# The last message pass of a two-layer graph transformer on one core: its softmax weights read from a PSUM bank instead of SBUF

## The reference

```
def _gat_conv(x, W, a_src, a_dst, b, src, dst, n):
    xw = x @ W
    e = jax.nn.leaky_relu((xw @ a_src)[src] + (xw @ a_dst)[dst], 0.2)
    m = jax.ops.segment_max(e, dst, num_segments=n)
    ex = jnp.exp(e - m[dst])
    s = jax.ops.segment_sum(ex, dst, num_segments=n)
    alpha = ex / (s[dst] + 1e-16)
    agg = jax.ops.segment_sum(alpha[:, None] * xw[src], dst, num_segments=n)
    return agg + b
```

## Time and profile before

| | us |
|---|---|
| median of 3 runs | 2983.78 |
| lowest, highest | 2980.12, 2986.76 |
| the profiled execution | 2979.18 |
| its span in the trace | 2977.4 |
| of it, from the first gather of the changed pass to its last sum | 2204.3 to 2726.2 |

### The profile page before, as it was taken

One profiled execution on the slowest core, in us unless ns is written; L12 is line 12 of the kernel. 1 busy time (PEld: TensorE's weight loads), 2 busy tenths in 40 slices (PEclk: granted clock), 3 DMA queues, 4 the chain that ended last, 5 costly groups with the idle time before them and its releaser, 6 DMA issues. The chain is left out here.

```text
span 2977.4 us, 42673 instructions
## 1 busy us (share of the span) xinstructions
PE 2298.1 (77%) x11382; PEld 1713.3 (58%) x11382; DVE 1399.9 (47%) x3453; ACT 1059.5 (36%) x2811; POOL 1403.0 (47%) x1426
## 2 busy tenths in 40 slices
PE   3899737766677988999994697876745988774996
PEld 3465324444445767888883465554534777553775
DVE  6655426666666230111115332342257666555677
ACT  2422224444442112332332443265412565442320
POOL 2122377777750042111110577777767777774300
PEclk8999858778888899999997898988865999997998
DMA  6256544444421014676663433343556444434001
GB/s 196 81 161 202 159 113 113 115 115 116 113 78 31 1 64 142 203 219 199 217 200 108 152 105 106 105 136 114 168 168 187 125 128 126 123 111 150 33 0 44
DMA packets 244440, 374.17 MB, mean 126 GB/s; under 512 B 66889, under 2 KB 179861, under 8 KB 244235
## 3 DMA queue, kind: packets, MB, share of 16 engines
q0 software_dynamic: 64624, 179.69, 21.0%
q1 hardware_dynamic: 132718, 140.75, 15.5%
q10 hardware_dynamic: 46892, 51.32, 5.2%
HBM read 301.77 MB, written 69.88 MB: 125 GB/s over the span
## 5 line engine op out<-in xcount | busy, mean ns | idle before, releaser
L2668 POOL DMA_INDIRECT cm_rows<-rows,e_bsrc x392 | 373.9, 954 | 202.5 <-issue 97.5
L1403 POOL DMA_INDIRECT at_rows<-values,e_brow x392 | 391.9, 1000 | 139.8 <-issue 92.0
L1132 POOL DMA_INDIRECT store<-rows,e_bsrc x392 | 397.3, 1013 | 119.5 <-issue 104.5
L1479 PE MATMUL at_part<-at_msg,store 128*128 128x265 f32 x880 | 272.5, 453 | 85.0 <-DVE at_msg L1634 49.9
L2804 PE MATMUL cm_part<-cm_rows,cm_one 128*128 x880 | 261.9, 440 | 91.9 <-SPq L2680 61.5
L1157 PE MATMUL banks<-ag_msg,ag_one 128*128 128x258 f32 x880 | 236.2, 405 | 85.6 <-issue 43.3
L2804 PEld LDWEIGHTS cm_part<-cm_rows,cm_one 128*128 128x128 f32 x880 | 180.2, 217 | 157.8 <-issue 133.9
L1479 PEld LDWEIGHTS at_part<-at_msg,store 128*128 128x128 f32 x880 | 179.1, 220 | 157.3 <-DVE at_msg L1634 81.4
L3019 DVE TENSOR_TENSOR store<-store,cm_part 128x256 f32 x220 | 92.2, 419 | 336.2 <-PE cm_part L2804 308.2
L1157 PEld LDWEIGHTS banks<-ag_msg,ag_one 128*128 128x128 f32 x880 | 167.1, 198 | 139.2 <-issue 55.7
L2105 POOL DMA_INDIRECT expert_out<-x_y,x_target x56 | 53.7, 959 | 370.5 <-DVE x_y L2208 363.1
(11 more groups left out here) (660 smaller groups left out, 3988.5 us busy)
## 6 DMA issues: line engine op xcount, KB each, us to landing
x_w<-in_L_ffn_W1p SPq DMA_DIRECT2D x32, 1024.0 KB, 5.2
x_w<-in_L_ffn_W2p SPq DMA_DIRECT2D x32, 1024.0 KB, 5.6
values<-p_hv ACTq DMA_DIRECT2D x25, 1088.0 KB, 4.9
p_brow<-local_row SPq DMA_DIRECT2D x44, 320.0 KB, 3.5
xn_acc<-low_row SPq DMA_DIRECT2D x28, 448.0 KB
expert_in<-z_z POOLq DMA_DIRECT2D x7, 1032.0 KB
je_y<-expert_out SPq DMA_DIRECT2D x25, 256.0 KB, 2.8
at_rows<-values,e_brow POOLq DMA_INDIRECT x392, 2.8
```

Source lines behind the costliest of these rows:

```text
L1132: pool.indirect_dma_start(rows[:, b % slots, k, :], None, table, bass.IndirectOffsetOnAxis(index[:, k, b:b + 1], 0)).then_inc(gathered[b % ...
L1403: pool.indirect_dma_start(rows[:, b % RING, k, :], None, table, bass.IndirectOffsetOnAxis(e.block_row[:, k, b:b + 1], 0)).then_inc(gathere ...
L1479: last = pe.matmul(part[:, n % deep, 0:wide], one[:, n // U % 2, k, n % U, :], msg[:, n % 4, k, :], start=(k == 0), stop=(k == K2 - 1))
L2668: pool.indirect_dma_start(rows[:, b % SLOTS, k, :], None, table, bass.IndirectOffsetOnAxis(e.block_src[:, k, b:b + 1], 0)).then_inc(gather ...
```

## The change

The edge weights stay in PSUM too. In `segment_softmax`, TensorE transposes channel 0 of `s` once more, into bank 2 (`small`), before the transposes that go to `scores`. The bank is handed to `aggregate` as `factors` (128 partitions, `k`, block). There the multiplication takes its second input from `factors` and no longer from `scores`. The copy of the two channels beside the row still reads `scores`.

```
                 if n >= 2:
                     pe.wait_ge(back_kept, n - 1)
+                for k in range(K2):
+                    pe.transpose(small[:, k * NB + h * BH:k * NB + (h + 1) * BH], s[:, h, 0, k * P:(k + 1) * P], c.ident[0:BH, 0:BH])
                 for j in range(step):
...
-    return (back_kept, len(steps)), turn
+    return (back_kept, len(steps)), turn, small[:, 0:K2 * NB].rearrange("p (k b) -> p k b", k=K2)
...
                 if flat:
                     dve.tensor_copy(msg[:, n % 4, :, D:wide], w)
-                    dve.tensor_tensor(msg[:, n % 4, :, 0:D], row, w[:, :, 0:1].broadcast_to([P, K2, D]), ALU.mult).then_inc(weighted, 1)
+                    dve.tensor_tensor(msg[:, n % 4, :, 0:D], row, factors[:, :, bass.ds(b, 1)].broadcast_to([P, K2, D]), ALU.mult).then_inc(weighted, 1)
...
-                    gate, down_ps = segment_softmax(nc, "sm2_", c, e, 1, 2, s2, source, scores, banks, *made)
-                    aggregate(nc, "ag2_", c, e, e.block_src, rows2, 1, scores, acc, store[:], banks, gate,
+                    gate, down_ps, factors = segment_softmax(nc, "sm2_", c, e, 1, 2, s2, source, scores, banks, *made)
+                    aggregate(nc, "ag2_", c, e, e.block_src, rows2, 1, scores, factors, acc, store[:], banks, gate,
```

More of the change, by code:

```diff
@@ L1099, in _, with aggregate @@
                     dve.tensor_tensor(s[:, h], fwd[:, h, 0:1, :].broadcast_to([BH, 2, BLK]), s[:, h], ALU.subtract).then_inc(shifted, 1)
-    return (back_kept, len(steps)), turn
+    return (back_kept, len(steps)), turn, small[:, 0:K2 * NB].rearrange("p (k b) -> p k b", k=K2)
 SLOTS = 14
 LAG = 5
-def aggregate(nc, tag, c, e, index, table, heads, weights, acc, ring, banks, gate, ride):
+def aggregate(nc, tag, c, e, index, table, heads, weights, factors, acc, ring, banks, gate, ride):
     width = table.shape[1]
```

## The result

The changed kernel takes 2961.88 us (median of 4 runs, 2958.71 to 2968.26) against 2982.08 us (4 runs, 2980.12 to 2986.76). The ratio is 0.9933, 95% interval 0.9912 to 0.9954. A second set of 6 runs gave 2960.85 us and 0.9933 (0.9920 to 0.9945). The forecast was 2963, 2955 to 2975. The profiled execution took 2958.71 us, its span 2956.2.

What follows compares the result with a forecast made beforehand. POOL's back-to-back gathers were taken as the bound; -19.1 us of holds and +0.04 us for the register operation sum to -19.1, giving 2960.1 from the profiled time or 2964.7 from the median; 2963 was taken, range 2955 to 2975.

Steps and rivals of the forecast that it cites:

- POOL as the bound: Gathers of the last pass: POOL issues them back to back, 1.25 us each undisturbed, and the last one sets the end.
- What holds a gather: Gathers starting inside the two-SBUF-input multiplication wait: 68 starts, 281 ns each on the mean; moving weights to PSUM gives -19.1 us.
- The multiplication's own duration: DVE multiplication with PSUM weights: 684 ns taken against 692, upper bound 1384 ns, no cost or gain expected.
- The register operation: One more on DVE's sequencer per message: 40 ns, 8.8 us in DVE's idle time, only +0.04 us on the path.
- the four transposes: Extra PE work before the pass: scores whole 0.46 us later, covered by DVE's clearing of the accumulator.
- The hold of the bias sum: The riding MLP's bias sum, two SBUF inputs, keeps holding gathers: 13 starts, 136 ns each, 1.8 us remaining.
- the lock stays: Rival: any long DVE multiplication reading the ring and writing SBUF holds POOL; no gain, 2980 to 2984 us, chance 0.06.
- the point from which a slower multiplication decides: DVE becomes the pass's bound if the multiplication takes 0.57 us more, 1.26 us.
- the upper bound that I allowed: Multiplication at double length, 1384 ns: DVE needs 466 us for the pass, giving 3015 to 3019 us.
- the slower case: Rival: a longer multiplication makes DVE the bound, 3015 from the profiled time or 3019 from the median; chance 0.02.
- half of it comes back: Rival: POOL gains, but late PE catch-up or late freed slots take 9.6 us, giving 2973 us; chance 0.08.
- PE's catching up: PE working off its backlog in the pass: 354.8 us busy against 413 us that stay, so POOL remains the bound.

Runs made afterwards that it cites:

- Half of the gathers: Changed kernel with only the k = 0 gathers of the pass, 196 of 392 left out, sums not the reference's: 2929.46 us, ratio 0.9836 to the kernel before.
- The transposes alone: Kernel before plus four PE transposes into bank 2, which nothing reads; the multiplication still takes its weights from SBUF: 2980.86 us, ratio 0.9997.
- exchanged inputs: Changed kernel with the multiplication's inputs swapped, PSUM weights first and gathered SBUF rows second: 2961.26 us in one run.
- the kernel with the step in both passes: Changed kernel with layer 0's attention weights also kept in PSUM, without ACT's copy to SBUF: 2944.14 us against 2960.85 for the changed kernel.
- the scalar pointer: Changed kernel with two 256-element tensor_scalar instructions, weight a per-partition SBUF scalar, instead of the multiplication; transposes unread: 2964.62 us, ratio 0.9946 to the kernel before.

## Why the prediction was right, and where it was not

- POOL as the bound, gather behind gather, with the end of the pass 6.4 us behind its last start: right. Half of the gathers makes the pass 28 us shorter, and in the kernels where POOL bounds the pass and I followed each gather, no gap before one is above 0.32 us.
- What holds a gather: right. -19.1 us was forecast for POOL's line. The holds in the pass went from 21.0 to 1.0 us, the stream of gathers is 19.4 us shorter, and the medians fell by 20.2 us in the first set and 18.8 in the second. The transposes alone gave nothing, and with exchanged inputs the gain is there as with the change.
- The multiplication's own duration: 684 ns, the value taken, from the row nearest in kind and with no row for a repeated PSUM number. The register operation is there with 40 ns, and the four transposes cost nothing that can be measured.
- The hold of the bias sum stays: right (1.8 us before, 0.8 us after, 7 starts instead of 13). No run shows why fewer start there: the second profile of the changed kernel has 7 too, the kernel with the step in both passes 12. This 1.0 us was not forecast.
- The rival "the lock stays": 80 starts inside the multiplication without a hold refute it. The sentence of the Trainium skill that stands beside it (SBUF — State Buffer, "Who interferes with whom") had a first measurement see no stall of DMAs from `tensor_tensor`, by a reason marked as inferred. For these gathers it does not hold with two SBUF inputs: 68 starts were 281 ns too long on the mean. By the other rule of that section of the Trainium skill (two SBUF inputs against an instruction that reads SBUF) the trace agrees, since a gather has its row numbers in SBUF; that this read is what waits is not shown, only that it fits.
- What failed is the reason given for a cost of nothing: "It costs or saves nothing either way at that size, because DVE is busy for only 121 of the second window's 222 us". At 684 ns the cost was nothing indeed, but DVE's idle time is not the room that it was taken for. A message passes from DVE to PE and its product comes back, and that loop needs 1.77 us a message with half of the gathers. DVE's instructions add up to 1.39 us; their records overlap, and by the windows of the earlier trace rows DVE is busy for (140.6 + 120.6) / 220 = 1.19 us. So the point from which a slower multiplication decides is not 0.57 us. If each added part counts in full, it is an estimated (434.7 - 388.7) / 220 = 0.21 us against the old time, and 0.13 us against the new one. The nearest run to the upper bound that I allowed is the one with each message multiplied twice, which adds 0.69 us and a wait: it took 3071 us, not 3015 to 3019. The forecast stood because the multiplication came out at 684 ns; the chance of 0.02 for the slower case rested on a price that was too low by some 50 us, and on a threshold nearly three times too high.
- The rival "half of it comes back" had PE's catching up as its mechanism. There were 434.7 - 388.7 = 46 us of room before the change, and 18 us of it are used now. It didn't come, but with 28 us to spare, about half of what PE's 354.8 us of busy time in 413 had made me think.

## What to carry to other kernels

Look at the duration of POOL's indirect gathers one by one: where the median is at the floor and the mean isn't, look in the timeline for the DVE instruction that is under way when the long ones start. Taking one of the two SBUF inputs of that instruction from PSUM ended the holds in both passes where it was done, in the last pass in either position, and a PSUM bank that was idle in that stage cost nothing. Judge a variant by the holds as well as by the time: the scalar pointer landed in the range expected of it by another way than its theory's. Before you call an added cost hidden in an engine's idle time, measure the pace of the loop in which it sits, by making the present bound cheap.

## What the runs showed of the hardware that was not expected

- A gather is held only if the DVE instruction is under way when it starts. One that starts ahead of it isn't: the gather of 2359.69 in the earlier trace rows took 0.95 us, though this multiplication of the kernel before began 0.20 us behind its start:

```profile
2359.89 0.69 DVE L1193 TENSOR_TENSOR ag_msg<-store,scores 128x512 f32 x1
```

- When both start at nearly the same moment, DVE is the one that waits. Before the change 11 of 220 multiplications took over 700 ns, up to 758. Beside each of them a gather started, from 0.02 us ahead to 0.04 us behind its start, and took 946 to 949 ns. After the change no multiplication takes more than 691 ns. From the kernel before:

```profile
2652.21 0.76 DVE L1193 TENSOR_TENSOR ag_msg<-store,scores 128x512 f32 x1
2652.24 0.95 POOL L1132 DMA_INDIRECT store<-rows,e_bsrc  x1 [0.30 <-issue]
```

- A `tensor_scalar` with one SBUF tensor and a scalar from SBUF still meets the gathers: 51 started inside one and were 68 ns longer on the mean, and 96 of its 440 instructions took over 400 ns against a median of 349, 91 of them ending 0.12 us behind a gather's end.
- A DVE read of PSUM that repeats one number 256 times costs no more than a dense one: 684 ns for 512 elements, as in the earlier trace rows.
